# GpSimd's sums of a recurrence step wait for the third part of the state in place of the state itself

## The reference

```python
def step(h, xt):                       # 64 steps, one after the other
    m = concat([xt, h]) @ weight + bias
    c = tanh(m[:, units:])
    g = sigmoid(m[:, :units] + 1.0)
    h_new = g * h + (1.0 - g) * c
x = x + ys                             # ys: all h_new
# gate from means of x over time, top 2 of 4 experts for each batch row
x = x + sum_e w[b, e] * mask[e] * expert_e(x) + shared_expert(x)
```

## Time and profile before

| | |
|---|---|
| median of 3 runs | 687.25 us (686.86 to 687.51) |
| the profiled execution's own time | 687.1 us |
| its span, first to last instruction | 685.3 us |
| mean granted TensorE clock | 0.988 |
| TensorE matmul busy | 643.7 us, 94% of the span |
| VectorE busy | 425.8 us, 62% |
| ScalarE busy | 289.8 us, 42% |
| GpSimd busy | 265.4 us, 39% |

### The profile page before, as it was taken

The page is one execution under the profiler, slowest core; times in us unless marked ns, Lnnn a source line. Parts: engine busy times, 40 slices in busy tenths (PEclk is TensorE's granted clock), DMA queues, the critical chain, the costliest instruction groups (busy, mean ns, idle before and its releaser), DMA issues.

```text
span 685.3 us, 16932 instructions
## 1 busy us (share of the span) xinstructions
PE 643.7 (94%) x5752; PEld 557.7 (81%) x5752; DVE 425.8 (62%) x942; ACT 289.8 (42%) x485; POOL 265.4 (39%) x531
## 2 busy tenths in 40 slices
PE   2779999999999999999999999999999999999990
PEld 2668888888888888888768888888888999999980
DVE  5798766665656656567766655555547875555453
ACT  3224433333333333333536544544446755544540
POOL 3576646454454554534344433113321343333000
PEclk9999999999999999999999999999999999999995
DMA  6521110000000000000002100000002300000014
GB/s 247 186 64 63 48 32 2 1 0 0 0 0 0 0 0 0 0 2 2 1 0 77 46 0 0 0 0 0 0 0 78 107 18 0 0 0 0 0 64 183
DMA packets 8037, 20.97 MB, mean 31 GB/s; under 512 B 960, under 2 KB 1216, under 8 KB 7488
## 3 DMA queue, kind: packets, MB, share of 16 engines
q1 hardware_dynamic: 7568, 19.64, 8.3%
q10 hardware_dynamic: 432, 0.85, 0.3%
HBM read 16.30 MB, written 4.19 MB: 30 GB/s over the span
## 4 chain that ended last, share of the span: by engine, by line
PE 87%; DVE 6%; DVEq 2%; issue 2%; DMA 1%; ACT 1%; SPq 0%; POOL 0%; ACTq 0%
PE zy L722 53%; PE hp L722 33%; DMA par<-in_small 1%; DVE h_r L421 1%; DVE acc L665 1%; DVEq L633 1%; DVEq L653 1%; DVE d_t L433 1%; DVEq L592 1%; ACT uc L313 1%; DVE shared_buf L595 1%; DVE h_b L423 0%; DVE d_t L431 0%; DVE h_b L436 0%; DVE acc L639 0%
## 5 line engine op out<-in xcount | busy, mean ns | idle before, releaser
L406 DVE TENSOR_TENSOR g_lo<-g_f,g_hi 128x512 fp32r<-128x512 f32 (+2 forms) x176 | 132.9, 755 | 127.7 <-ACT g_hi L327 121.2
L322 ACT ACTIVATE g_f<-hp,par 128x512 f32<-128x512 f32 (+2 forms) x184 | 123.4, 670 | 176.5 <-PE hp L722 174.5
L722 PE MATMUL zy<-g_hi,w_buf 128*128 128x512 f32 (+2 forms) x736 | 190.7, 381 | 0.0
L722 PE MATMUL hp<-shared_buf,w_buf 128*128 (+1 forms) x720 | 173.6, 376 | 1.3 <-DVE shared_buf L595 1.3
L327 ACT ACTIVATE g_hi<-g_f 128x512 fp32r<-128x512 f32 (+2 forms) x184 | 112.9, 613 | 123.5 <-PE zy L722 123.3
L722 PEld LDWEIGHTS zy<-g_hi,w_buf 128*128 128x128 f32 x736 | 138.2, 188 | 22.7
L722 PEld LDWEIGHTS hp<-shared_buf,w_buf 128*128 128x128 f32 x720 | 135.0, 188 | 20.8 <-issue 1.9
L722 PEld LDWEIGHTS zy<-h_b,y_all 128*128 128x128 bf16 x3072 | 94.1, 98 | 27.2 <-issue 15.1
L722 PE MATMUL zy<-h_b,y_all 128*128 128x64 bf16 x3072 | 103.3, 193 | 9.4 <-DVE h_b L436 6.1
L722 PE MATMUL zy<-g_lo,w_buf 128*128 128x512 f32 (+2 forms) x368 | 110.3, 381 | 0.0
L722 PE MATMUL hp<-x_hl,w_buf 128*128 (+1 forms) x384 | 99.8, 395 | 0.3 <-POOL x_hl L254 0.3
(11 more groups left out here) (109 smaller groups left out, 433.7 us busy)
## 6 DMA issues: line engine op xcount, KB each, us to landing
stage<-in_w_exp SPq DMA_DIRECT2D x40, 256.0 KB, 2.8
out_y<-acc SPq DMA_DIRECT2D x2, 1376.0 KB, 5.0
acc<-in_x SPq DMA_DIRECT2D x1, 2048.0 KB, 9.1
acc<-in_x SPq DMA_DIRECT2D x1, 1536.0 KB, 9.8
out_y<-acc SPq DMA_DIRECT2D x1, 1344.0 KB, 5.1
acc<-in_w SPq DMA_DIRECT2D x1, 512.0 KB, 4.2
acc<-in_x SPq DMA_DIRECT2D x1, 512.0 KB, 7.2
acc<-in_w ACTq DMA_DIRECT2D x1, 512.0 KB, 5.0
```

What stands on the lines that cost most here:

```text
L322: act.activation(g_f[:, j % 2, 0:n], hp[j % 2][:, 0:n], ACT.Gelu_apprx_tanh, bias=par[:, S_B1 + e * NCH + j:S_B1 + e * NCH + j + 1]).then_ ...
L406: dve.tensor_tensor(g_lo[:, j % 2, 0:n], g_f[:, j % 2, 0:n], g_hi[:, j % 2, 0:n].bitcast(F32), ALU.subtract).then_inc(glo_done, 1)
L722: return pe.matmul(out_, lhsT=lhsT, rhs=rhs, start=start, stop=stop, skip_group_check=True)
```

## The change

In `add_h` GpSimd waits for `h3_done` in place of `h_done`. Both semaphores count one for each step and both stand at s + 2 behind step s, so the threshold is the same number. `h3_done` is raised by L425, the last of the three instructions that split the state; `h_done` by L440, the instruction ahead of them.

```diff
                 sg = seg[:, bass.ds((s * 3 + 2) // 64, 1)].rearrange("p s k b -> p (s k) b")
-                pool.wait_ge(h_done, s + 2)
+                pool.wait_ge(h3_done, s + 2)
                 pool.tensor_tensor(hi, a, h_f[:, 1 - i % 2], ALU.add).then_inc(x1_hi, 1)
                 pool.tensor_tensor(a, a, h_f[:, 1 - i % 2], ALU.add).then_inc(x1_sum, 1)
```

## The result

The changed kernel takes 690.08 us (median of 8 runs, 688.62 to 691.25) against 687.08 us before (8 runs, 686.46 to 687.66): a ratio of 1.0044, 95% interval 1.0032 to 1.0055, or +3.0 us (+2.2 to +3.8). That lies above the forecast of 688.3 and above its range. The profiled execution took 691.05 us with a span of 689.3 us, 4.0 more than the span of before. Three terms make up those 4.0 us, and each can be read from the traces: the start of group 2, the wait behind step 63 and the clock behind that wait.

A forecast was written before the change was run, and what follows sets the result against it. A dependent loop bounds steps 1 to 7, full TensorE 61.6 to 321.7 us. Front -0.3 plus end +1.45 gives +1.15 on profiled 687.1, 688.25; with the median's 0.15, 688.4, stated as 688.3 us, range 686.9 to 689.2.

The forecast's parts named there:

- Steps 0 to 7: Step 0 gains 0.58 us; in steps 1 to 7 collisions move, -0.03 us a turn, -0.2 us over seven.
- Step 0: First step: L421, L423 and L425 run alone and TensorE's parts start earlier, -0.58 us.
- the walk: Rule for who holds the resource shared by VectorE and GpSimd, stepped through a turn: 3.92 us before, 3.89 changed.
- Step 8: TensorE's first layer finds its cover for L254 of step 7 used up: a new wait of 0.57 us.
- Steps 9 to 10: VectorE has L406 and L414 and is nearly full; collisions falling elsewhere leave about -0.1 us.
- the front: Sum of the terms for steps 0 to 10: -0.3 us, bounds -0.85 and +0.2.
- Steps 11 to 62: TensorE stays full; at a group's start 0.6 us or more is left before x1_done is late: cost 0.
- Behind step 63: x1_done has no cover; L406 goes ahead of L254 and TensorE starts later: +1.45 us, bounds +0.9 and +1.55.
- The gate: Its means wait for seg_done; L516 ends at 332.4, TensorE arrives at 333.4: no second wait.
- Rival B: Slower: heavier collisions in a turn's front half, 0.3 us more per turn, +2.1 over seven, 690.5 us; chance 0.13.

The follow-up runs named there:

- first_group: Kernel before with only steps 0 to 7 waiting for h3_done; 686.29 against 686.74 us, ratio 0.9995.
- middle_groups: Kernel before with only steps 8 to 55 waiting for h3_done; 687.78 against 686.74 us, ratio 1.0011.
- remainder_first: Changed kernel with L406 of each group's last step, from group 2 on, waiting until L254 is through; 689.35 against 686.74 us for the kernel before.
- after_swap: Changed kernel with TensorE doing a second-layer chunk before its x1_done wait behind step 63; 688.81 against 686.87 us for the kernel before.
- last_group: Kernel before with only steps 56 to 63 waiting for h3_done; 688.97 against 686.59 us, ratio 1.0029.
- after_again: The changed kernel, unchanged, measured again against the kernel before; 690.11 against 686.74 us, ratio 1.0043.
- after: The changed kernel in its first measurement, against the kernel before; 690.08 against 687.08 us, profiled execution 691.05 us.

## Why the prediction was wrong

Two things failed: the cover that the prediction gave TensorE at a group's start, which was used up at step 16, and the clock behind step 63, which it had not priced. The time would lie above the range even without the clock: +2.5 us on 687.25 is 689.8, and the range ended at 689.2.

**Steps 0 to 7: right.** Step 0 gave -0.55 (said: -0.58), and the turn came out at 3.91 us (said: 3.89). The walk's durations for L431 to L414 (0.40, 0.51, 0.44, 0.38, 0.44, 0.22, 0.29, 0.68) are all within 0.03 us of the trace, and L251's 0.83 is 0.84. The sum had -0.2 us for seven turns and the trace has 0.0: the sum set the walk's 3.89 against the walk's own 3.92 and not against the 3.90 of the trace.

**Step 8: right.** A new wait for `x1_done`, 0.41 us against 0.57. The steps fell back by 0.64 us there (by 0.55 in first_group), more than the wait by itself.

**Steps 9 to 10: wrong in sign.** The term "about -0.1" should have brought the front to -0.3; the steps stand at +0.10 by step 9, at +0.48 by step 11, and at +0.24 by step 16. In these steps VectorE's chain holds TensorE, and L436 of step 9 met L241 (0.57 us against 0.29 before). VectorE's L406 and L414 ahead of step 11 take longer too, 1.01 and 0.94 us against 0.94 and 0.77; that this is the rest of the +0.48 is my reading. L436 of step 9:

```profile
57.07 0.57 DVE L436 SCALAR_TENSOR_TENSOR h_b<-d_t,uc 128x128 bf16<-128x128 f32 x1
...
57.04 0.46 POOL L241 TENSOR_TENSOR x_hl<-acc,x_hl  x1 [0.18 <-POOL x_hl L239]
...
57.70 1.73 PE L722 MATMUL zy<-h_b,y_all 128*128 128x64 bf16 x48 [0.74 <-DVE h_b L436]
```

**Steps 11 to 62: this step failed.** I priced them at 0, with "0.6 us or more left" at each group's start, read from a step of a later group. Group 1 isn't like it: it has L414 as well. Timeline of step 15 of the changed kernel:

```profile
88.41 0.29 DVE L425 TENSOR_TENSOR h_b<-h_r,h_b 128x128 bf16<-128x128 f32 x1
89.22 0.69 DVE L406 TENSOR_TENSOR g_lo<-g_f,g_hi 128x512 fp32r<-128x512 f32 x1 [0.52 <-ACT g_hi L327]
89.83 0.95 DVE L414 TENSOR_TENSOR w_buf<-stage,w_buf 128x512 fp32r<-128x512 f32 x1
...
88.90 0.46 POOL L251 TENSOR_TENSOR x_hl<-acc,h_f 128x128 f32 x1 [1.90 <-DVE h_b L425]
89.32 0.91 POOL L252 TENSOR_TENSOR acc<-acc,h_f 128x128 f32 x1
90.42 0.68 POOL L254 TENSOR_TENSOR x_hl<-acc,x_hl  x1 [0.19 <-POOL acc L252]
...
91.34 1.65 PE L722 MATMUL hp<-x_hl,w_buf 128*128 x6 [0.56 <-POOL x_hl L254]
```

In the kernel before, L251 of this step starts at 86.86. It is 2.04 us later here, not 1.3. 0.70 of it is that L440 itself ends later, at 87.36 against 86.66, since the step starts 0.14 later and its L431 and L436 take 0.55 and 0.58 us against 0.28 and 0.29. The other 1.34 us lies between the ends of L440 and L425, 0.47 of it idle time of VectorE ahead of L421 (it stands there in the kernel before too). Then L252 is 0.45 us longer beside L406, and L254 0.22 longer beside L414, than the 0.46 us that they take alone. L254 ends at 91.10, against 88.52 before, 2.58 us later. TensorE needed it at 90.52 in the kernel before: the cover was 2.0 us here and not the 2.4 read from the ordinary step. It is used up, TensorE waits, and step 17 is another 0.8 us later. first_group and middle_groups put it there; that L406 and L414 make the difference is read from this trace, not from an experiment. The front was thus +1.05 and not -0.3 us, 0.54 of the miss by step 16 and 0.81 at step 17. For groups 2 to 6 the price 0 was right.

**Behind step 63: right in place, order and size, the size partly by luck.** I said +1.45 us with L406 ahead of L254; it was +1.47. But L254 started 0.10 us later than I had it, and L406 held it up by 0.37 us and not by 0.5, as its 0.82 against 0.45 us and remainder_first show. The two errors cancel.

**The gate: right.** L516 is no second wait in the changed kernel; with after_swap it becomes one of 0.41 us.

**What no step had: the clock.** The prediction named a wait of 1.9 us and said of the clock only that it is 1.00 in the stretches of before. Nothing in that trace excluded a fall after a longer wait, and I gave it neither a rival nor a price. It costs 1.55 us in an execution that has it: 6 of 11 in last_group, 4 of 7 in after_again, and at least 3 of the 8 of the first measurement. Rival B had the time (690.5) by luck: its heavier collisions in the turns did not come.

The sum with what was measured is +1.05 + 1.47 + 1.55 = +4.07 us for an execution with the fall, and +2.5 without. The median of +3.0 lies between them.

## What to carry to other kernels

Two engines that hold each other up are worth walking through operation by operation: such a walk gave the durations of VectorE's eight instructions of a turn to 0.03 us here. But it must be done for every kind of step, and the last step of the group with the most work is the one to check first; cover read from an ordinary step is no bound for it. Moving work later within a full turn only moved the collisions here; taking work out of the turns is what gained. A wait of TensorE is priced by its length plus what the clock loses behind it.

## What the runs showed of the hardware

- After TensorE stood still for 1.82 us the granted clock fell to 0.5 in some executions and not in others of the same kernel (6 of 11 in last_group, 4 of 7 in after_again). The three traces that have the fall (after, after_again, last_group) agree on its shape: the clock is still 1.00 when the matmuls start again, falls 0.14, 0.41 and 0.81 us later, and stays at 0.5 for 3.4 us in each. The gate's matmuls behind it are 1.55 to 1.57 us later for it in all three. No trace here shows a fall after a wait of 0.3 to 0.6 us at this place, nor after the one of 1.45 us, nor after the waits of 1.3 or 1.4 us for L595 in eleven traces.
- One part of the scatter of 1 to 3 us is a single instruction of VectorE in the chain behind the gate, and by the traces it is a collision with GpSimd again. L595 runs eight times; min, median and max in ns, in the kernel before and then in first_group:

```profile
L595 DVE CAST shared_buf<-x_hl x8: 433/450/1514, 351.1 to 354.7; 128x256 fp32r x8
```

```profile
L595 DVE CAST shared_buf<-x_hl x8: 425/456/472, 350.9 to 353.6; 128x256 fp32r x8
```

GpSimd's L283 runs beside them. In the timeline of the kernel before, and then of first_group:

```profile
352.22 1.51 DVE L595 CAST shared_buf<-x_hl 128x256 fp32r x1
...
352.11 1.34 POOL L283 TENSOR_TENSOR g_lo<-g_f,g_hi 128x512 fp32r<-128x512 f32 x1 [1.44 <-ACT g_hi L327]
```

```profile
351.97 3.24 POOL L283 TENSOR_TENSOR g_lo<-g_f,g_hi 128x512 fp32r<-128x512 f32 x1 [1.44 <-ACT g_hi L327]
```

Either L283 gets in, takes 1.34 to 1.40 us, and one L595 takes 1.51 us; or the eight L595 pass at 0.45 us each and L283 takes 3.23 to 3.26 us. All 14 traces are of one kind or the other, 11 of the first and 3 of the second (first_group, after_again, remainder_first). In the first kind TensorE waits 1.3 or 1.4 us for L595, in the second 0.4. Together with the clock this gives last_group's three levels; that the 1.2 us between the upper two are this collision is inferred from the size. What decides who gets in first stays open: L283 starts 1.00 to 1.06 us behind the first L595 in the traces of the first kind and 1.02 or 1.03 us behind it in those of the second.
